# A recommender tower on one core: h rolled by one copied to PSUM, three remainders a chunk on GpSimd, and x_base of the second chunk in an idle slot

## What is computed

```python
e = stack([tbl_f[ids[:, f]] for f in range(32)], axis=1)          # (1024, 32, 32)
h = e
for i, (W, b) in enumerate(((W0, b0), (W1, b1), (W2, b2))):         # 128, 128 and 1 outputs
    z = relu(einsum('bhd,bmd,ohm->bod', h, e, W.reshape(O, H, 32)) + b)
    h, direct = (z[:, :64], z[:, 64:]) if i < 2 else (None, z)      # direct parts are kept
h = concat([concat(directs, 1).sum(-1), dense_ctx], axis=1)          # (1024, 145)
y = relu(relu(h @ W_top1 + b_top1) @ W_top2 + b_top2) @ W_top3
```

## Time and profile before

| | us |
|---|---|
| median of 3 runs | 1128.2 (1127.32 to 1129.06) |
| the profiled execution | 1127.21 |
| its span, first to last instruction | 1125.4 |
| PE busy | 1086.0 (97%) |
| DVE busy | 1034.8 (92%) |
| POOL busy | 744.1 (66%) |
| ACT busy | 597.8 (53%) |

### The profile page before, as it was taken

The page is one execution under the profiler, slowest core; times in us unless marked ns, Lnnn a source line. Parts: engine busy times, 40 slices in busy tenths (PEclk is TensorE's granted clock), DMA queues, the critical chain, the costliest instruction groups (busy, mean ns, idle before and its releaser), DMA issues.

```text
span 1125.4 us, 11475 instructions
## 1 busy us (share of the span) xinstructions
PE 1086.0 (97%) x3562; PEld 660.5 (59%) x3562; DVE 1034.8 (92%) x580; ACT 597.8 (53%) x517; POOL 744.1 (66%) x333
## 2 busy tenths in 40 slices
PE   3789999999999999999999999999999999999997
PEld 1355655666565666656666666656665666656665
DVE  1589999999999999999999999999999999999993
ACT  0156555545654555565455556555545655555545
POOL 6466767777787777768777777877777787743110
PEclk9899999999999999999999999999999999999999
DMA  6665454665544466554446555544566554455200
GB/s 203 206 166 147 141 144 132 177 174 153 149 147 135 129 177 176 166 143 138 141 128 171 176 155 161 141 134 127 169 176 168 148 142 145 131 153 145 78 0 1
DMA packets 73576, 162.97 MB, mean 145 GB/s; under 512 B 14785, under 2 KB 39874, under 8 KB 73554
## 3 DMA queue, kind: packets, MB, share of 16 engines
q1 hardware_dynamic: 52738, 147.57, 46.2%
q10 hardware_dynamic: 12624, 10.92, 3.0%
q0 software_dynamic: 8192, 4.21, 2.3%
HBM read 95.52 MB, written 8.39 MB: 92 GB/s over the span
## 4 chain that ended last, share of the span: by engine, by line
PE 86%; DVE 6%; issue 2%; ACT 1%; DMA 1%; another core or an unknown queue 1%; ACTq 1%; POOL 1%; SPq 0%; DVEq 0%; POOLq 0%
PE z_ps L723 84%; DVE raw L591 2%; PE u_ps L723 2%; DVE prod L527 2%; DVE prod_lo L597 2%; DMA twice<-raw 1%; POOL gathered L364 1%; ACTq L1016 0%; ACT prod_hi L1097 0%; ACT h_roll L1083 0%; PE mlp_ps L723 0%; ACT h L969 0%; DMA gathered<-in_table,rows_sb 0%; DMA base_sb<-in_row_base 0%
## 5 line engine op out<-in xcount | busy, mean ns | idle before, releaser
L723 PE MATMUL z_ps<-prod,w_sb 128*128 128x512 f32 x1280 | 575.6, 596 | 10.8 <-ACT direct L959 4.0
L364 POOL DMA_INDIRECT gathered<-in_table,rows_sb x256 | 454.1, 1774 | 73.9 <-issue 68.3
L723 PEld LDWEIGHTS z_ps<-prod,w_sb 128*128 128x128 f32 x1280 | 243.6, 191 | 273.4 <-issue 262.3
L986 ACT CAST prod_hi<-raw 128x2048 fp32r<-128x2048 f32 x160 | 305.2, 1908 | 180.0 <-DVE raw L591 179.3
L591 DVE TENSOR_TENSOR raw<-h_roll,x_roll 128x2048 f32<-128x2048 f32 x160 | 363.4, 2288 | 1.2
L527 DVE TENSOR_TENSOR prod<-mlp_ps,x_roll 128x2048 f32<-128x2048 f32 x124 | 279.6, 2285 | 8.5 <-issue 5.7
L723 PE MATMUL z_ps<-prod_hi,w_hi 128*128 128x512 f32 x648 | 249.0, 464 | 3.5 <-DVE prod_lo L597 3.1
L375 POOL TENSOR_TENSOR prod_lo<-raw,prod_hi 128x2048 fp32r<-128x2048 f32 x32 | 146.8, 4587 | 135.4 <-DVE prod_lo L597 109.1
L597 DVE TENSOR_TENSOR prod_lo<-raw,prod_hi 128x2048 fp32r<-128x2048 f32 x98 | 223.9, 2286 | 1.0
L384 POOL TENSOR_TENSOR prod_lo<-raw,prod_hi 128x2048 fp32r<-128x2048 f32 x30 | 139.0, 4632 | 122.3 <-DVE prod_lo L597 122.3
L723 PE MATMUL z_ps<-prod_lo,w_hi 128*128 128x512 f32 x648 | 204.8, 396 | 0.0
(11 more groups left out here) (71 smaller groups left out, 329.5 us busy)
## 6 DMA issues: line engine op xcount, KB each, us to landing
x_roll<-x_dram SPq DMA_DIRECT2D x128, 512.0 KB
x_base<-x_dram SPq DMA_DIRECT2D x32, 512.0 KB
h_roll<-h_roll SPq DMA_DIRECT2D x32, 448.0 KB
h_roll<-h_roll SPq DMA_DIRECT2D x32, 384.0 KB
h_roll<-h_roll SPq DMA_DIRECT2D x32, 320.0 KB, 6.0
x_dram<-gathered SPq DMA_DIRECT2D x64, 128.0 KB
twice<-raw ACTq DMA_DIRECT2D x128, 64.0 KB
h_roll<-h_roll SPq DMA_DIRECT2D x32, 192.0 KB, 7.0
```

Of the source, the lines that this page charges most:

```text
L364: nc.gpsimd.indirect_dma_start(gathered[:, u, g * DIM:(g + 1) * DIM], None, table, bass.IndirectOffsetOnAxis(ap=rows_sb[:, col:col + 1], a ...
L723: return nc.tensor.matmul(*args, **kw)
L986: nc.scalar.copy(prod_hi[:, SPLIT_SLOT[r], :, :], raw[:, RAW_SLOT[r], :, :]).then_inc(hi_ready, 1)
```

## The change

A1, which was one split, and L1a, which was one whole, become two splits **A10** and **A12**: roll 1 of h with rolls 0 and 1 of x, and with rolls 2 and 3. So a step has 2 + 2 wholes and 6 splits in place of 2 + 3 and 5. Roll 1 of h is copied to `mlp_ps` by ScalarE (`copy_h1`, after the two products of layer 1 that read h itself there), and A10 and A12 read it there. `raw` gets a third slot. GpSimd makes three remainders, lo B0, lo B2 and lo B3, with 2, 3 and 3 gathers between them; VectorE makes lo B1, lo A10 and lo A12. The lists of all engines are written anew; SP issues the rolls of h after the fourth `x_roll`, rolls 2 and 3 ahead of roll 1; product16 comes after raw B1. The `x_base` of chunk 1 goes into `raw[:, 0, 0, :]` at once. To make room, `x_part16` and `h2` have one buffer, and the weights of the MLP are loaded late into a part of `x_roll`.

```diff
-WHOLE1 = 3
-B0, B1, A1, B2, B3 = range(5)
-SPLIT1 = 5
+WHOLE1 = 2
+B0, B1, B2, A10, A12, B3 = range(6)
+SPLIT1 = 6
-SPLIT_SLOT = (0, 1, 2, 0, 1)
+SPLIT_SLOT = (0, 1, 2, 0, 1, 2)
-RAW_SLOT = (0, 1, 0, 1, 0)
-RAW_RING = 2
+RAW_SLOT = (1, 2, 0, 1, 2, 0)
+RAW_RING = 3
...
 GpSimd
-            def lo1(c):
...
-            def lo3(c):
+            def lo(c, r, window, opened, ready):
...
+                pool.wait_ge(hi_ready, rounded)
+                pool.wait_ge(window, opened)
+                nc.gpsimd.tensor_tensor(prod_lo[:, SPLIT_SLOT[r], :, :], raw[:, RAW_SLOT[r], :, :],
+                                        prod_hi[:, SPLIT_SLOT[r], :, :], ALU.subtract).then_inc(ready, 1)
...
-                    lo3(c - 1)
+                    lo(c - 1, B3, lo_ready, lo_count(c - 1, A12), lo3_ready)
...
+                    gather(*after, range(0, 2))
...
+                    lo(c, B0, raw16_ready, c + 2, lo0_ready)
...
+                    gather(*after, range(2, 5))
...
+                    lo(c, B2, lo16_ready, c + 2, lo2_ready)
...
+                    gather(*after, range(5, GATHERS))
...
 SP
-                for a in range(1, ROLLS):
+                for a in (2, 3, 1):
...
+                to = x_base1 if isinstance(c, int) and c == 1 else x_base[:, :]
...
-                        if reuses:
-                            roll_h(c - 1, 1 - s)
...
+                if reuses:
+                    roll_h(c - 1, 1 - s)
...
 VectorE
+                if r == A10:
+                    dve.wait_ge(h1_copied, c + 1)
+                    dve.wait_ge(lo0_ready, c + 1)
+                elif r == A12:
+                    dve.wait_ge(lo_ready, lo_count(c, B1))
+                elif r == B3:
+                    dve.wait_ge(lo2_ready, c + 1)
...
                 split_product(c, u, B0)
-                if not is_first(c):
-                    rolled_once()
                 split_product(c, u, B1)
                 if not is_last(c):
-                    split_rest16(c + 1)
-                split_rest(c, B0)
+                    product16(c + 1, (u + 1) % UNROLL, group if u < UNROLL - 1 else group + 1)
                 dve.wait_ge(h0_copied, c + 1)
                 for k in range(PAIRS0):
-                    whole(first1(c) + 1 + k, slot1(c, u) + 1 + k, twice(mlp_ps[:, :]),
+                    whole(first1(c) + k, slot1(c, u) + k, twice(mlp_ps[:, :]),
                           x_roll[:, s, k * PAIR:(k + 1) * PAIR, :])
                 if not_first(c):
+                    sum_direct(c - 1, *before)
+                split_product(c, u, B2)
+                split_rest(c, B1)
+                if not is_last(c):
+                    split_rest16(c + 1)
+                split_product(c, u, A10)
+                split_product(c, u, A12)
+                if not_first(c):
                     layer2(c - 1, *before)
-                    sum_direct(c - 1, *before)
-                split_product(c, u, A1)
-                split_product(c, u, B2)
-                split_rest(c, A1)
                 split_product(c, u, B3)
-                split_rest(c, B2)
+                split_rest(c, A10)
+                split_rest(c, A12)
...
 TensorE
                 layer1(c, u, 0)
+                layer1(c, u, 1)
+                split(z1_of(c), c, B0)
                 if not is_last(c):
                     layer0_pairs16(c + 1)
-                    if not_first(c):
-                        layer2_u(c - 1, (u - 1) % UNROLL)
-                split(z1_of(c), c, B0)
...
-                layer1(c, u, 1)
+                if not_first(c):
+                    layer2_u(c - 1, (u - 1) % UNROLL)
                 split(z1_of(c), c, B1)
-                layer1(c, u, 2)
-                split(z1_of(c), c, A1)
+                split(z1_of(c), c, B2)
+                split(z1_of(c), c, A10)
                 if u == 0 and not_first(c):
                     layer2_sum(c, group - 1)
-                split(z1_of(c), c, B2)
+                split(z1_of(c), c, A12)
...
 ScalarE
+            def copy_h1(c, u):
+                s = u % 2
+
+                act.wait_ge(h1_rolled[s][0], (c - s + 2) * 16)
+                act.wait_ge(prod_ready, first1(c) + WHOLE1)
+                nc.scalar.copy(mlp_ps[:, :], h_roll[:, s, 1, :]).then_inc(h1_copied, 1)
...
+                round_products(c, B0)
+                if not_first(c):
+                    relu1(c - 1, (u - 1) % UNROLL)
                 if not is_last(c):
                     double_pairs16(c + 1)
-                round_products(c, B0)
+                round_products(c, B1)
+                copy_h1(c, u)
                 if not is_last(c):
                     round_pairs16(c + 1)
-                if not_first(c):
-                    relu1(c - 1, (u - 1) % UNROLL)
-                round_products(c, B1)
+                round_products(c, B2)
+                round_products(c, A10)
                 if not is_last(c):
                     relu0(c + 1, (u + 1) % UNROLL)
-                round_products(c, A1)
...
+                round_products(c, A12)
```

More of the change, by code:

```diff
@@ L192, in build_tower @@
         top_b = x_base
+        x_base1 = raw[:, 0, 0, :]
         early = h_roll[:, 1, :, :].rearrange("p a (t n) -> p (a t) n", n=P)
@@ L353, in make_rows, with gather @@
                                         ALU.add).then_inc(rows_made, 1)
-            def gather(c, u, group, part):
+            def gather(c, u, group, columns):
                 made = settled(pool, group + 1)
@@ L361, in gather @@
                 wait(pool, late_copied, freed)
-                for g in range(part * GATHERS // 2, (part + 1) * GATHERS // 2):
+                for g in columns:
                     col = u * GATHERS + g
@@ L391, in step @@
                 if not_first(c) and pool_makes_lo3(c - 1 if isinstance(c, int) else c):
-                    lo3(c - 1)
+                    lo(c - 1, B3, lo_ready, lo_count(c - 1, A12), lo3_ready)
                 ahead = UNROLL - 1
                 more = not isinstance(c, int) or c + ahead < CHUNKS
+                after = c + ahead, (u + ahead) % UNROLL, group if u == 0 else group + 1
                 if more:
@@ L397, in step @@
                         make_rows(group + 1)
-                    gather(c + ahead, (u + ahead) % UNROLL, group if u == 0 else group + 1, 0)
-                lo1(c)
-                if more:
-                    gather(c + ahead, (u + ahead) % UNROLL, group if u == 0 else group + 1, 1)
+                    gather(*after, range(0, 2))
+                if is_last(c):
+                    lo(c, B0, raw_ready, c * SPLIT1 + B1 + 1, lo0_ready)
+                else:
+                    lo(c, B0, raw16_ready, c + 2, lo0_ready)
+                if more:
+                    gather(*after, range(2, 5))
+                if is_last(c):
+                    lo(c, B2, lo_ready, lo_count(c, B1), lo2_ready)
+                else:
+                    lo(c, B2, lo16_ready, c + 2, lo2_ready)
+                if more:
+                    gather(*after, range(5, GATHERS))
             make_rows(0)
             for c in range(UNROLL - 1):
-                for part in range(2):
-                    gather(c, c, 0, part)
+                gather(c, c, 0, range(GATHERS))
             over_chunks(pool, step)
@@ L543, in products0 @@
                 copied = not_first(c, 2)
+                base = mlp_ps[:, :] if copied else x_base[:, :] if is_first(c) else x_base1
                 if copied:
@@ L558, in products0 @@
                         dve.wait_ge(x_roll_loaded[s][b], (c - s + 2) * 8)
-                    whole(first0(c) + k, slot0(c, u) + k, twice((mlp_ps if copied else x_base)[:, :]), x_roll[:, s, k * PAIR:(k + 1) * PAIR, :])
-                if not is_first(c):
-                    product16(c, u, group)
+                    whole(first0(c) + k, slot0(c, u) + k, twice(base), x_roll[:, s, k * PAIR:(k + 1) * PAIR, :])
             def split_rest16(c):
@@ L1044, in step @@
                 round_products(c, B3)
+                if not is_last(c):
+                    copy_late(c + 1, (u + 1) % UNROLL, group if u < UNROLL - 1 else group + 1)
                 if u == 0 and not_first(c):
```

144 lines of the change are left out of this document (61 added, 83 removed).

## The result

The changed kernel takes 1180.0 us (median; 1177.36 to 1182.34), the kernel before, run beside it, 1127.8: a ratio of 1.0462, 95% interval 1.043 to 1.0494. It is slower, as forecast, but by 52 us and not by 26, and outside the range of 1138 to 1174.

The account below looks back on a forecast made before the run. TensorE was taken to bound the kernel before at 32.51 us a step, the new loop the changed one at 33.46. Steps +22.5, start +1.5, end +2.2: +26.2 on 1127.2, 1153.4; median 1.0 above, so 1154, range 1138 to 1174.

Parts of the forecast that it names:

- TensorE's own work: On TensorE, a whole of 3.44 us becomes a split of 2.80: 0.64 less a step, if nothing holds it.
- VectorE's own work: On VectorE, thirteen instructions of about 2.20 us before and thirteen after: cost 0.
- The new loop: L0a to L0b on TensorE, VectorE from L1b to lo A10, then A10 and A12: 33.46 us a step, 0.95 above 32.51.
- Rolls of h: Issued after raw B3, landing 5.2 to 7.0 us later; raw B0 has 1.8 to spare, so cost taken as 0.
- The third rival: Raw B0 late: rolls of h behind a 512 KB load; each us beyond the spare 1.8 costs 29; chance 0.08.
- Ends: Start and end of the run, outside the 29 steps: +1.5 us at the start and +2.2 at the end.
- GpSimd against raw B0: lo B3 on GpSimd overlaps raw B0 by about 0.8 us; about 0.5 lost, inside the spare 1.8.
- What the profile would show: Steps of about 33.5 us, a gap of 1.5 to 2 at L1b and of about 1.5 before A10.
- the sign of late rolls: A gap in front of raw B0 ended by a DMA, listed among what would show the forecast wrong.

Follow-up runs that it names:

- e1: Changed kernel without the DMAs of rolls 2 and 3 of h, and the waits for them, after the third chunk: 1156.7 us, ratio 1.0257.
- e7: Changed kernel with half of each load of x_roll left out from the fourth chunk on, same order of issue: 1156.4 us, ratio 1.0279.
- e9: Kernel before with the x_base part of the change alone: 1125.9 us, ratio 0.9987.
- e4: Changed kernel with rolls 2 and 3 of h dropped and GpSimd's remainders halved: 1155.2 us, ratio 1.0245.
- e3: Changed kernel with half of each of GpSimd's three remainders left out after the third chunk: 1169.1 us, ratio 1.0383.
- e2: Changed kernel with rolls 2 and 3 of h issued between the third and the fourth x_roll load: 1236.4 us, ratio 1.0935.
- e8: Changed kernel, all work kept, with the order changed on four engines and rolls 2 and 3 issued earlier: 1259.5 us, ratio 1.1192.
- e11: Changed kernel, all work kept, with roll 1 of h issued after raw B0: 1164.0 us, ratio 1.033.

## Why the prediction was right and where it failed

- *TensorE's own work and VectorE's own work*: VectorE's is right (DVE 1035.1 against 1034.8). TensorE's busy time was to fall by 29 x 0.64, 18.6; it falls by 2.9 in the kernel after (1083.1 against 1086.0), by 11.5 in e1 (1074.5) and by 15.3 in e7 (1070.7). Why it stays so high in the full kernel was not traced. TensorE is not what sets the step there, and the terms of it that stand in the loop came out as read (L0a to L0b is 6.23 in e1, 82.83 to 89.06).
- *The new loop*, 33.46 a step: right. With the rolls gone (e1), or half of the loads (e7), the step is 33.70 and 33.69 (e7's L0a rows start at 82.27 and 1059.38), 0.08 from the forecast with layer2_sum. Those runs take 1156.7 and 1156.4; the forecast was 1154.
- *Rolls of h* ("issued after the fourth `x_roll`, that is after raw B3 at 25.5, and land 5.2 to 7.0 after issue ... I take 0"): this step failed. It let the rolls land 5.2 to 7.0 us after raw B3, where its own times had room for 10.8 (34.5 - 25.5, and 1.8 to spare). In the step shown above they land 11.8 after it, 1.0 too late. Two sizes were wrong. The issuing was put at nothing: behind raw B3, SP issues the fourth load and three pieces of rolls before the second piece of roll 3, which costs 3.3 us. And the earlier trace rows is line 425, the first pieces alone; VectorE waits for the second pieces too (line 426), whose row in the kernel before is

```profile
DMA to landing us min/median/max: 5.5/7.0/8.8
```

  In the kernel after, the second piece of roll 3 lands 8.50 after its issue in the step shown and 7.21 to 9.05 in the chain's other steps from 179 us on, of which these are the shortest and the longest:

```profile
318.69 7.21 DMA h_roll<-h_roll
...
455.24 9.05 DMA h_roll<-h_roll
```

  It lands so late at the end of a stream that fills the DMA engines for 12 us, with four loads ahead in place of two; with half of the bytes of these loads (e7) it is 4.4 to 6.5. The term that was put at 0 is 34.47 - 33.70 = 0.77 us a step, 22 us in 29 steps.
- The third rival said just this, with the right place and about the right price (29 us for each us past the slack, so 1183 for one), at a chance of 0.08. What it set against itself, "7.0 is the longest landing seen", holds for the first pieces only: the second had taken up to 8.8. A sum of bytes would have shown it as well. By the prediction's own times raw A10 ends at 20.6 and raw B0 is wanted at 34.5. Four loads and two rolls of 512 KB in 13.9 us are 226 GB/s; with `x_part16` (128 KB) and roll 1, which are in the same stream, they are 3.8 MB and 273 GB/s. The four full windows above deliver 236 to 326, 267.5 in the mean (measured only after the change). By this estimate nothing is to spare.
- *Ends*: +0.8 against +1.5 in the head, +2.6 against +2.2 in the tail: right. The x_base part was put at nothing by itself, and e9 shows so.
- *GpSimd against raw B0*: the direction was right and it is inside the slack in the loop without rolls (e4 gains hardly more than 1 us on e1). About 0.5 a step was reckoned; VectorE's raw products from h_roll take 311.9 us in e1 and 292.3 in e4, with GpSimd's remainders halved, which is 0.7 a step. Taking half of the overlap was too small. A row of the kernel after, at another product, and GpSimd's remainder beside it:

```profile
646.51 3.04 DVE L593 TENSOR_TENSOR raw<-h_roll,x_roll 128x2048 f32<-128x2048 f32 x1
```

```profile
642.83 4.56 POOL L377 TENSOR_TENSOR prod_lo<-raw,prod_hi 128x2048 fp32r<-128x2048 f32 x1
```

  The remainder runs 0.88 into raw B2 (to 647.39) and raw B2 takes 3.04 in place of 2.29: 0.75 lost. With the loop through the rolls such losses count: in e3 these products take 3.1 us less in all than in the kernel after (290.7 for 293.8) and wait 4.7 less for GpSimd (2.6 for 7.3), which is 7.8 of e3's 11. The rest was not traced.
- *What the profile would show*: a gap at L1b, one at A10, none at raw B0. Right for e1 and e7; in the full kernel the gap at A10 is there (0.88 at 626.45), and that of L1b moved to raw B0, ended by a DMA, which the prediction had named as the sign of late rolls.

So the direction came from a loop that is there, and not from luck; the size was missed by a second loop that was listed and given too small a chance. What stays open: how bytes behind the rolls delay them, and whether an order exists that keeps both loops short.

## What to carry to other kernels

When a change moves reads of a double buffer later, add up what then has to happen between the last read and the first use: the issuing of each transfer that stands ahead on the queue, and all bytes of the stream at the rate of a full queue. A landing time read from the old order is not enough, least of all that of a piece that doesn't land last. A wait taken away by moving a transfer ahead of another returns at the one that was passed (e2), so sum the whole burst first. Before a short VectorE instruction with two SBUF operands is moved, look at what GpSimd does at the new place.

## What the runs showed of the hardware

- A VectorE instruction with both operands in SBUF that starts during a GpSimd subtraction waits for its end: 0.41 became 3.11 us, 0.69 became 3.01 (e8), and 2.29 became 3.04 where the subtraction had 0.88 left (kernel after).
- On a full queue the stretches in which, by the bytes moved so far, mostly rolls from SBUF to SBUF are left run at 236 and 245 GB/s, the stretch of the loads from DRAM at 326 (kernel after). The two kinds were not measured apart.
- The second piece of roll 3 (192 KB), issued behind four loads and three other pieces, landed 7.21 to 9.05 us after its issue. Each issue on SP took 0.54 to 1.14 us in the chain shown, so the place of a transfer in the list costs time before a byte moves.
- 512 KB issued behind a transfer on the same queue delayed it: the waits for rolls 2 and 3 fell from 54.7 to 34.0 us when roll 1 was issued later (e11).
